# A fused two-block transformer on one core: stack DMAs by parts, banks of maxima and x moved, and the order of the front and of self attention

## The reference

```
# block 0: cross attention with adaptive norm
xq  = (1+scale_q(cond)) * norm(x)   + bias_q(cond)
xkv = (1+scale_k(cond)) * norm(ctx) + bias_k(cond)
x   = x + mha(xq@Wq+bq, xkv@Wk+bk, xkv@Wv+bv) @ Wp + bp
# block 1: self attention, cross attention, MLP
h = norm(x)*(1+scale_msa) + shift_msa
x = x + (mha(q, k, v of h@qkv_w + qkv_b) @ self_o_w + self_o_b) * gate_msa
h = norm(x)*g2 + b2
x = x + mha(h@q_w+q_b, ctx@k_w+k_b, ctx@v_w+v_b) @ cross_o_w + cross_o_b
h = norm(x)*(1+scale_mlp) + shift_mlp
x = x + (gelu(h@w1+b1) @ w2 + b2) * gate_mlp
```

## Time and profile before

| what | value |
|---|---|
| time, median of 3 runs | 539.46 us (538.98 to 542.21) |
| the profiled execution | 543.47 us, span 541.7 us |
| mean granted TensorE clock | 0.911 |
| busy share: PE, VectorE, ScalarE, GpSimd | 85%, 54%, 46%, 34% |
| first exp of attention 0 | about 57.7 us |
| first cross layer | 57.7 to 257.5 us |
| self layer | 257.5 to 340.9 us |
| second cross layer | 340.9 to 482.1 us |
| MLP | 482.1 us to the end |

### The profile page before, as it was taken

The page is one execution under the profiler, slowest core; times in us unless marked ns, Lnnn a source line. Parts: engine busy times, 40 slices in busy tenths (PEclk is TensorE's granted clock), DMA queues, the critical chain, the costliest instruction groups (busy, mean ns, idle before and its releaser), DMA issues.

```text
span 541.7 us, 11662 instructions
## 1 busy us (share of the span) xinstructions
PE 457.9 (85%) x4306; PEld 325.8 (60%) x4306; DVE 290.5 (54%) x784; ACT 250.3 (46%) x555; POOL 183.7 (34%) x245
## 2 busy tenths in 40 slices
PE   5765778989899879879797867898988987999996
PEld 5532454657575456556665644566656655678995
DVE  7717447471847544633766738745653543644321
ACT  1442455643555536555442323566665654572221
POOL 3233133463245425525141404244333413243200
PEclk9968698987999979999886868999999989999999
DMA  8667953472334275656817020746174032110000
GB/s 227 163 109 113 220 119 74 104 152 68 52 96 82 57 127 92 89 90 84 111 50 90 10 44 19 191 111 100 33 119 92 17 73 85 30 45 17 19 17 18
DMA packets 48927, 46.13 MB, mean 85 GB/s; under 512 B 12767, under 2 KB 47071, under 8 KB 48871
## 3 DMA queue, kind: packets, MB, share of 16 engines
q1 hardware_dynamic: 45951, 45.12, 42.8%
q10 hardware_dynamic: 2920, 0.27, 0.5%
HBM read 14.57 MB, written 0.93 MB: 29 GB/s over the span
## 4 chain that ended last, share of the span: by engine, by line
PE 60%; DVE 12%; issue 12%; ACT 6%; DMA 4%; POOL 3%; SPq 2%; ACTq 0%; POOLq 0%; DVEq 0%
PE bank L443 8%; PE bank L451 7%; DVE nmax L929 7%; PE bank L582 7%; PE bank L545 6%; PE bank L562 6%; PE bank L477 5%; PE bank L633 5%; PE bank L622 5%; PE bank L607 2%; PE bank L595 2%; ACT xt L683 2%; PE bank L500 2%; ACT prob L774 2%; DMA q_stack_all<-nm_t 2%
## 5 line engine op out<-in xcount | busy, mean ns | idle before, releaser
L929 DVE TENSOR_REDUCE nmax<-bank 112x1 f32<-112x375 f32 (+1 forms) x288 | 141.9, 549 | 101.8 <-PE bank L545 101.1
L774 ACT ACTIVATE prob<-bank 128x448 f32<-128x448 f32 (+2 forms) x224 | 116.4, 544 | 80.0 <-PE bank L562 75.5
L545 PE MATMUL bank<-k_stack,q_stack_all 96*128 96x375 bf16 x256 | 68.1, 350 | 24.0 <-issue 10.8
L1068 POOL TENSOR_TENSOR fill_space<-fill_space 128x375 f32<-128x375 f32 x32 | 29.9, 934 | 117.3 <-ACT fill_space L706 117.3
L562 PE MATMUL bank<-q_stack_all,k_stack 99*128 99x112 bf16 x768 | 55.7, 217 | 7.0 <-DMA q_stack_all<-nm_t 6.9
L451 PE MATMUL bank<-wkv,fill_space 128*128 128x256 f32 (+1 forms) x192 | 53.2, 418 | 9.5 <-ACT xt L683 7.1
L545 PEld LDWEIGHTS bank<-k_stack,q_stack_all 96*128 96x128 bf16 x256 | 24.6, 103 | 58.1 <-DVE nmax L929 21.8
L443 PE MATMUL bank<-fill_space,wkv 128*128 128x375 f32 x128 | 54.6, 555 | 3.1 <-ACT fill_space L706 2.3
L582 PE MATMUL bank<-prob,v_tokens 128*17 128x112 f32 (+1 forms) x1536 | 57.0, 266 | 0.1
L562 PEld LDWEIGHTS bank<-q_stack_all,k_stack 99*128 99x128 bf16 x768 | 41.7, 100 | 24.7 <-issue 13.4
L1082 POOL TENSOR_TENSOR v_tokens<-v_tokens,bias_rows_v 128x256 f32<-128x256 f32 (+1 forms) x48 | 33.5, 713 | 44.4 <-ACT v_tokens L718 44.4
(11 more groups left out here) (120 smaller groups left out, 687.9 us busy)
## 6 DMA issues: line engine op xcount, KB each, us to landing
k_stack<-fill_space SPq DMA_DIRECT2D x192, 93.8 KB, 3.5
q_stack_all<-q_part SPq DMA_DIRECT2D x72, 112.0 KB, 4.2
k_stack_all<-ctx_norm SPq DMA_DIRECT2D x24, 112.0 KB, 5.0
k_stack_all<-in_L_xcond_mlp_w_dram SPq DMA_DIRECT2D x2, 1024.0 KB, 7.8
...
```

Of the source, the lines that this page charges most:

```text
L545: last = pe.matmul(to[:, o:o + w], q_all[0:DEEP, q + h * N2:q + h * N2 + P], keys, start=True, stop=True)
L774: act.activation(prob[n % 4][0:rows, :], bank[SCORE_T[n % 2]][0:rows, 0:GH * T], ACT.Exp).then_inc(exp_done, 1)
L929: dve.tensor_reduce(nmax[:, g * hs:(g + 1) * hs], bank[SCORE[n % 3]][0:T, 0:hs * w].rearrange("t (h k) -> t h k", k=w), AX_X, ALU.max, neg ...
L1068: pool.tensor_tensor(kr[:, m, :], kf[:, m, :], kp[i % 2][:, 0, m, :], ALU.subtract).then_inc(krest_done, 1)
```

## The change

Five edits, none of which adds or drops arithmetic:

1. load_k and d wait part by part: the three DMAs of the high part go once the high part is there, then the two of the middle, then the low one.
2. In a cross attention the steps k stand at units 3 and 5 instead of 4 and 6, and D of half 0 at unit 6 instead of 7.
3. X of pairs 2 to 5 goes from bank CX to TB, at unit 7 instead of 6 (behind V in the list).
4. The maxima's transpose (all but those of attentions 10 to 15) goes into the score bank that is next in the ring; PE waits until that bank's group before has been read, and the next group in it waits for the maxima's copy.
5. The front is reordered and some of its T and K steps get banks 0, 1 and 3; loads 4 (contexts 4 to 7) comes before D(1). In the self layer X, Q, Kp, Vp, h, m, d of pair 7 come later, those of pair 8 earlier; B(9) one place earlier.

```diff
@@ -130,13 +130,13 @@
...
     for n, s in enumerate([
-            [("A", 0), ("cA", 0), ("order", -1), ("B", 0), ("cB", 0), ("mods", 0), ("mods", 1), ("X", 0), ("T", 0, 0), ("T", 0, 1),
-             ("order", 0), ("A", 1), ("cA", 1), ("B", 1), ("cB", 1)],
-            [("Q", 0), ("K", 0, 0), ("h", 0, "q"), ("K", 0, 1), ("m", 0, "q"), ("k", 0, 0), ("k", 0, 1), ("X", 1), ("T", 1, 0), ("T", 1, 1),
-             ("d", 0, "q"), ("D", 0, 0), ("D", 0, 1), ("cA", 2)],
+            [("A", 0), ("cA", 0), ("order", -1), ("B", 0), ("mods", 0), ("X", 0), ("cB", 0), ("mods", 1), ("Q", 0), ("T", 0, 0), ("T", 0, 1),
+             ("order", 0), ("h", 0, "q"), ("A", 1), ("cA", 1), ("m", 0, "q"), ("B", 1), ("cB", 1)],
+            [("K", 0, 0), ("K", 0, 1), ("k", 0, 0), ("k", 0, 1), ("X", 1), ("T", 1, 0), ("T", 1, 1),
+             ("d", 0, "q"), ("D", 0, 0), ("D", 0, 1), ("loads", 4), ("cA", 2)],
...
-             ("n", 0), ("d", 1, "q"), ("loads", 4)],
+             ("n", 0), ("d", 1, "q")],
             [("T", 2, 0), ("N", 0), ("L", 0), ("T", 2, 1), ("cA", 3)]]):
@@ -152,8 +152,8 @@
...
                     put(a, u, "K", i + 2, u // 2)
-                if u in (4, 6) and i + 2 < 2 * B:
-                    put(a, u, "k", i + 2, (u - 4) // 2)
+                if u in (3, 5) and i + 2 < 2 * B:
+                    put(a, u, "k", i + 2, (u - 3) // 2)
                 if u in (7, 9) and i + 1 < 2 * B:
@@ -171,7 +171,7 @@
...
                     put(a, u, "cB", i + 3)
-                if u in (7, 12) and i + 2 < 2 * B:
+                if u in (6, 12) and i + 2 < 2 * B:
                     put(a, u, "D", i + 2, u // 12)
@@ -186,25 +186,25 @@
...
-    (1, 2): [("A", 2)], (1, 4): [("B", 2)], (1, 6): [("X", 2)], (1, 9): [("Q", 2)], (1, 11): [("h", 2, "q")],
+    (1, 2): [("A", 2)], (1, 4): [("B", 2)], (1, 7): [("X", 2)], (1, 9): [("Q", 2)], (1, 11): [("h", 2, "q")],
     (2, 0): [("m", 2, "q")], (2, 3): [("d", 2, "q")],
-    (2, 2): [("A", 3)], (2, 4): [("B", 3), ("order", 1)], (2, 6): [("X", 3)], (2, 9): [("Q", 3)], (2, 11): [("h", 3, "q"), ("mods", 2)],
+    (2, 2): [("A", 3)], (2, 4): [("B", 3), ("order", 1)], (2, 7): [("X", 3)], (2, 9): [("Q", 3)], (2, 11): [("h", 3, "q"), ("mods", 2)],
     (3, 0): [("m", 3, "q")], (3, 3): [("d", 3, "q")],
-    (3, 2): [("A", 4)], (3, 4): [("B", 4)], (3, 6): [("X", 4)], (3, 9): [("Q", 4)], (3, 11): [("h", 4, "q")], (3, 12): [("Kp", 4)],
+    (3, 2): [("A", 4)], (3, 4): [("B", 4)], (3, 7): [("X", 4)], (3, 9): [("Q", 4)], (3, 11): [("h", 4, "q")], (3, 12): [("Kp", 4)],
...
     (5, 0): [("h", 4, "k")], (5, 2): [("m", 4, "k"), ("A", 5)], (5, 5): [("d", 4, "k")],
-    (5, 4): [("B", 5)], (5, 6): [("X", 5)], (5, 9): [("Q", 5)], (5, 11): [("h", 5, "q")], (5, 12): [("Kp", 5)],
+    (5, 4): [("B", 5)], (5, 7): [("X", 5)], (5, 9): [("Q", 5)], (5, 11): [("h", 5, "q")], (5, 12): [("Kp", 5)],
...
     (8, 4): [("A", 7)],
-    (9, 0): [("B", 7)], (9, 1): [("X", 7)], (9, 2): [("Q", 7)], (9, 4): [("Kp", 7), ("h", 7, "q")],
-    (10, 0): [("h", 7, "k")], (10, 1): [("Vp", 7), ("m", 7, "q"), ("d", 7, "q")], (10, 2): [("m", 7, "k"), ("d", 7, "k")],
-    (11, 0): [("A", 8)], (11, 2): [("B", 8)], (11, 4): [("X", 8)], (12, 2): [("Q", 8)], (12, 4): [("h", 8, "q")],
-    (13, 1): [("m", 8, "q"), ("d", 8, "q")],
-    (13, 0): [("A", 9)], (13, 2): [("B", 9)], (13, 4): [("X", 9)],
+    (9, 0): [("B", 7)], (9, 3): [("X", 7)], (10, 0): [("Q", 7)], (10, 2): [("Kp", 7), ("h", 7, "q")],
+    (10, 3): [("h", 7, "k")], (10, 4): [("Vp", 7), ("m", 7, "q"), ("d", 7, "q")], (11, 0): [("m", 7, "k"), ("d", 7, "k"), ("A", 8)],
+    (11, 1): [("B", 8)], (11, 3): [("X", 8)], (12, 0): [("Q", 8)], (12, 2): [("h", 8, "q")],
+    (12, 4): [("m", 8, "q"), ("d", 8, "q")],
+    (13, 0): [("A", 9)], (13, 1): [("B", 9)], (13, 4): [("X", 9)],
@@ -217,13 +217,15 @@
...
 BANK_OF = {("X", 0): 0, ("Q", 0): 1, ("X", 1): 2, ("Q", 1): 3, ("mods", 0): 7, ("mods", 1): TB,
-              ("Q", 2): TB, ("Q", 3): TB, ("Q", 4): TB, ("Kp", 4): TB, ("Q", 5): TB, ("Kp", 5): TB, ("Q", 10): TB, ("Q", 11): TB}
+              ("T", 0, 1): 3, ("K", 0, 1): 0, ("T", 1, 1): 3, ("K", 1, 1): 1,
+              ("X", 2): TB, ("Q", 2): TB, ("X", 3): TB, ("Q", 3): TB, ("X", 4): TB, ("Q", 4): TB, ("Kp", 4): TB,
+              ("X", 5): TB, ("Q", 5): TB, ("Kp", 5): TB, ("Q", 10): TB, ("Q", 11): TB}
...
-    uses, filled, read, maxima, tails = {}, {}, {}, {}, 0
+    uses, filled, read, maxima, tails, groups, ring = {}, {}, {}, {}, 0, 0, {}
@@ -236,20 +238,24 @@
...
-            elif step[0] == "N" and B + 2 <= step[1] <= 2 * B:
+            elif step[0] == "S":
+                groups += step[3] - step[2]
+            elif step[0] == "N" and B + 2 <= step[1] < 2 * B:
                 uses[step] = (CX, filled[CX], read[CX], 0, maxima.get(CX, 0), 0)
                 maxima[CX] = step[1] + 1
-            elif step[0] == "N" or step[0] == "tail" and step[2] == 0:
+            elif step[0] == "N":
+                uses[step] = (SCORE[groups % 3], 0, 0, 0, 0, 0)
+                ring[groups] = step[1] + 1
+            elif step[0] == "tail" and step[2] == 0:
                 uses[step] = (TB, filled.get(TB, 0), read.get(TB, 0), 0, maxima.get(TB, 0), tails)
-                maxima[TB] = step[1] + 1 if step[0] == "N" else maxima[TB]
             tails += step[0] == "tail" and step[2] == 2
-    uses["tail", NA - 1, 0] = (TB, filled[TB], read[TB], 0, maxima[TB], tails)
+    uses["tail", NA - 1, 0] = (TB, filled[TB], read[TB], 0, maxima.get(TB, 0), tails)
     for n in (13, 14, 15):
         use(("X", n), jobs_in(n))
-    return uses, filled, read
-USES, FILLED, READ = count_uses()
+    return uses, filled, read, ring
+USES, FILLED, READ, RING = count_uses()
@@ -439,6 +445,8 @@
...
                 pe.wait_ge(wkv_ordered, CH * (i // B + 1))
+                if USES["T", i, 1][0] != bk:
+                    read_by(pe, ("T", i, 1))
             for c in range(CH):
@@ -509,6 +517,8 @@
...
             a = step[1]
+            if bk in SCORE:
+                wait(pe, max_done, [g for g in RING if RING[g] >= a + 1][0] - 2)
             pe.wait_ge(nm_step, 4 * a + 4)
@@ -537,6 +547,7 @@
...
             wait(pe, max_done, n - 2)
+            wait(pe, nm_done, RING.get(n, 0))
             to = bank[SCORE[n % 3]]
@@ -943,7 +954,7 @@
...
             wait(dve, nm_in[a % 2], 16 * (a // 2))
-            src = cx[0:3 * H, CH * T:CH * T + T // 2].bitcast(BF16)
+            src = bank[USES[step][0]][0:3 * H, CH * T:CH * T + T // 2].bitcast(BF16)
             dve.tensor_copy(nm_t[a % 2][:, :], src).then_inc(nm_done, 1)
@@ -1061,7 +1072,7 @@
...
             _, i, m = step
-            pool.wait_ge(read[CX], USES[step][2] + 1)
+            read_by(pool, step)
             wait(pool, ksplit[m], 3 * i)
@@ -1151,13 +1162,20 @@
...
     def load_k(eng, i, half):
-        for m in range(CH):
-            eng.wait_ge(ksplit[m], 3 * (i + 1))
         lo, hi = half * P // HB, (half + 1) * P // HB
         at, to = half * H // HB * L, (half + 1) * H // HB * L
-        for s, w in enumerate(TERMS_K):
-            eng.dma_start(k_st[i % 2][s * D:(s + 1) * D, at:to].rearrange("d (h n) -> d h n", n=CH * L),
-                          kp[i % 2][lo:hi, w, :, :].rearrange("p c n -> p (c n)")).then_inc(kstacked[i % 2][half], 16)
+        for w in range(3):
+            if w == 0:
+                for m in range(CH):
+                    read_by(eng, ("K", i, m))
+            elif w == 1:
+                eng.wait_ge(kmid_done, CH * (i + 1))
+            else:
+                for m in range(CH):
+                    eng.wait_ge(ksplit[m], 3 * (i + 1))
+            for s in [s for s in range(NTERM) if TERMS_K[s] == w]:
+                eng.dma_start(k_st[i % 2][s * D:(s + 1) * D, at:to].rearrange("d (h n) -> d h n", n=CH * L),
+                              kp[i % 2][lo:hi, w, :, :].rearrange("p c n -> p (c n)")).then_inc(kstacked[i % 2][half], 16)
@@ -1174,12 +1192,12 @@
...
             to, terms = (q_all, TERMS_Q) if k == "q" else (k_all, TERMS_K)
-            sp.wait_ge(low_done[k], kinds_no(n, k) + 1)
             if k == "q" and l > 0:
...
                 sp.wait_ge(filled[CX], USES["gates", 0][1] + 1)
-            for t, w in enumerate(terms):
+            for w, t in [(w, t) for w in range(3) for t in range(NTERM) if terms[t] == w]:
+                sp.wait_ge((high_done, mid_done, low_done)[w][k], kinds_no(n, k) + 1)
```

## The result

The changed kernel takes 523.09 us (median of 4 runs, 520.37 to 526.35) against 539.22 us of the kernel before, a ratio of 0.969 (0.962 to 0.977). The forecast was 498 us, 487 to 517. The gain is 16 us, not 41. The profiled execution took 521.28 us, its span is 519.5 us. Medians are of all runs and ratios of those within 1.5% of the fastest; the profiled executions of experiments 3 and 12 were not among these, so their stage times lie high.

A forecast was written before the change was run, and what follows sets the result against it. TensorE was taken as nearly the bound, with time to win only from its idle gaps and its clock. Gains of 13.3 + 4.3 + 12.2 + 12.8 + 4.5 - 2.0 = 45.1 us off 543.5 gave 498 us, range 487 to 517.

The forecast's parts named there:

- Half 0's parts: Second cross layer: earlier stack DMAs end five score waits, 8.2 us, and give back 5.1 us of clock, 13.3 in all.
- k one place up: Conversions ahead of exp 4 and exp 6 delay them in each of 14 attentions: a cost of 2 us, bounds 0 and 7.
- The slower rival: ScalarE stalls on k at unit 5, waiting for a late GpSimd difference: time 552, chance 0.04.
- Attention 1's wait of 2.60 us: First cross layer, wait at 76.78: goes as the stack leaves earlier, 4.3 us with its clock.
- Half 1: K stack's second half lands at +4.5 us, its reader head 8 comes at +5.2 at the earliest: 0.7 us of room.
- I leave it so: Front: the maxima's DMA, 5.82 us from 51.28 with SyncE's queue full, was kept at that length.
- 4.5 us for the new order: Front: new step order and banks start stack DMAs about three us earlier; gain 4.5 us, bounds 2 and 7.
- The self layer: Pair 7's move gains 5.7 and loses 1.0 us, pair 8's gains 4.7 of wait and 3.4 of clock: 12.8.
- The terms for pair 7's move: Self layer: x's 2.33 us wait and 3.4 of clock go, 5.7 us; a later stack loses 1.0.
- The banks: x in the tail's bank ends four waits of V on xt, 7.1 us plus 5.1 of clock: 12.2; maxima's transpose at nothing.
- The second rival: Self-layer scores wait 4 us for pair 7's stack, clock falls, half 1's room is short: 9 us, time 507, chance 0.15.
- The first rival: Waits go but the clock does not come back, half clock falls elsewhere: 18.7 us lost, time 517, chance 0.16.

The follow-up runs named there:

- experiment 3: Kernel before plus only the stack DMAs waiting part by part, k at units 3 and 5, and D of half 0 at unit 6: 522.84 us, 0.970.
- experiment 12: The kernel of experiment 11 plus, in attention 22, head 8 of the next scores one unit later: 503.12 us, 0.934 of the kernel before.
- experiment 15: The kernel of experiment 12 with k back at units 4 and 6 and the first D at unit 7: 501.72 us, 0.934 of the kernel before.
- experiment 4: Kernel before plus only the stack DMAs waiting part by part, no step moved: 525.88 us, 0.974.
- experiment 5: Kernel before with only loads 4 moved in front of D(1): 543.5 us, 1.010.
- experiment 2: Changed kernel, loads 4 at its old place but waiting for attention 0's maxima to land, MLP weights for attention 16's: 519.37 us, 0.967 of the kernel before.
- experiment 11: Changed kernel, old self-layer order, only context 4 early, d(1) and contexts 5-7 behind attention 0's maxima, loads 1 and 2 later, MLP weights behind attention 16's: 505.42 us.
- experiment 10: Kernel before plus only the front's new order and its T and K banks, loads 4 at its old place: 537.78 us, 0.998.
- experiment 14: The kernel of experiment 12 with the front's order and its T and K banks as in the kernel before: 502.2 us, 0.934 of the kernel before.
- experiment 8: Changed kernel with the self-layer steps of pairs 7, 8 and 9 at their old places: 515.68 us, 0.959 of the kernel before.
- experiment 9: Changed kernel with pair 7's self-layer steps at their old places, pairs 8 and 9 at the new: 518.21 us, 0.965 of the kernel before.
- experiment 13: The kernel of experiment 12 with x of pairs 2 to 5 back at unit 6 in the bank shared with V: 510.73 us, 0.945 of the kernel before.

## Why the prediction was wrong, step by step

**Half 0's parts: right.** All five waits of 8.2 us are gone, DMAs leave as worked out (6.7 us from the attention's head, forecast 7.5), and the clock of the stretches behind them is back. The waits at the heads of attentions 17 to 22 are in no kernel that has the parts.

**k one place up: 2.0 forecast, not to be seen.** Experiment 15 against 12, and 3 against 4, lie within each other's intervals, which would hide a cost of this size. The slower rival, ScalarE stalled by GpSimd, did not come up.

**Attention 1's wait of 2.60 us: right.** By the parts alone the attention takes 4.4 us less (experiment 4), forecast 4.3; after, with the banks, it takes 21.0 us instead of 27.5. That the whole first cross layer comes within 0.9 us of its forecast is luck in part: PE's idle time fell by 6.3 us where 9.7 were forecast, and its busy time, by the clock, fell by 8.3 where 6.8 were.

**Half 1: the next wait in line, right in place, wrong in where it decides.** The text gave it 0.7 us of room and took it at no cost. In attentions 17 to 21 that holds. In 22, which has no K to make for a later context, the first units run faster: head 8's scores come at +3.8 us, the half lands at +5.1. The wait is 1.35 us, and 3.4 us of work is lost to half clock around it. Experiment 12 gives back 1.9 us of attention 22. This and the maxima of attention 16 are why the clock of the layer stays at 0.96, one of the prediction's signs of being wrong.

**The front: the step that failed most.** It is "I leave it so": the 5.82 us of the maxima's DMA was taken over as a constant, and it became 11.72. That number was read correctly as a wait behind SyncE's full queue; but the edits change just that queue. Loads 4 go early (experiment 5: 11.56 us, and 5.5 us slower by itself), and even without that the parts let SyncE run ahead, so that the contexts' loads get in front of the maxima (experiment 4: 9.14 us). This is 5.9 us at attention 0. The 7 us for the loads' transfer and the landing of D(1) by 53 were wrong with it: beside the stack DMAs the contexts' packets ran from 36.4 to 51.0, and the last packet of D(1) went at 58.2. No engine waited for that stack itself, but the maxima stood behind it. At attention 16 the same cause costs 3.0 us in attention 15 and 2.3 in 16 (34.0 to 28.7 in experiments 2 and 11). The other half of the step, 4.5 us for the new order, was 0.6 (experiments 10 and 14): the walk took away PE's wait for the bank and did not ask whether VectorE, behind it, had the time. It had work for 9.4 of the 10 us, and PE waited 4.4 us for it.

**The self layer: 12.8 forecast, 5.7 measured.** The terms for pair 8 are about right and come by the parts alone (experiment 4: attention 14 is 6.8 us shorter, forecast 8.1). The same parts took 3.7 us off attention 12, by an earlier stack of pair 7 in the old order, where the text kept a loss. The terms for pair 7's move have the wrong sign. The wait of 2.33 us for x went, yet the step did not name what queues behind B(7) on VectorE: B(7) kept its place ahead of N and the maxima, and with x later PE reaches the next scores first and waits 2.73 us for them. Q(7) and Q(8) stand ahead of N in the shared bank, which costs 0.88 us twice, behind ScalarE's q_full. All the moves together cost 4.4 us of the stage, 7 of the median (experiment 8); how they share it is open (experiment 9). The 1.0 us for a late stack of pair 7 didn't come.

**The banks: 12.2 forecast, 7.6 to 9 by the medians.** In the four attentions it is 8.1 to 10.8 us (experiment 13 against 11, 12, 14 and 15). The waits for xt are nearly as large as stated (7.1 us before, 6.2 in experiment 13), and the 5.1 us of clock lie within what the profiles show (3.1 to 6.6 in these attentions). What was put at nothing is the maxima's transpose: without the wait for xt PE comes to it sooner, VectorE's last split of the maxima doesn't, and PE waits 0.71, 0.52 and 0.52 us for it in attentions 1, 2 and 3, none of which is there before or in experiment 13. The term was also read from a profile with more half clock than the median run: alone on the kernel before, the edit gave 5.7 us (2.6 to 8.8).

**The sum.** Maxima's DMAs 5.9 + 3.0 + 2.3 = 11.2, the front's order 3.9, the self layer's order 4.4, half 1 about 2: 21.5 of the 22.9 us between the span forecast (496.6) and the span of after (519.5). The front's order is a gain that never was; the other three have repairs. With all three (experiment 15) the span is 501.8 us, without that for half 1 (experiment 11) 502.3, 5 to 6 us from the forecast. That these kernels come so near is luck in part: their maxima's DMA takes 2.4 us, where the forecast kept 5.8, and their self layer of 70.9 to 73.9 us has the old order, where the forecast's 70.6 was for the new.

**The rivals.** The second rival (a new wait in the self layer and at half 1, 9 us) is near in size, 4.4 + 2, but the cause that it names in the self layer is a late stack, and the runs show late maxima: near by luck. None of them had the maxima's DMA, though its row stood in the prediction, costed as a constant. The first rival, whose 517 us is the nearest of all to the result, is not what happened: where the waits went, the clock came back (0.96 from 0.92 in the first cross layer after the change, 0.99 in the second of experiment 11).

By the Trainium skill (DMA: Bandwidth & Descriptors, Queues, rings and completion order) each DMA engine changes between the queues it has work for, a packet at a time, so the backlog of SyncE's queue would not hold up ScalarE's. The runs disagree: the first packet of attention 0's maxima came 1.5 us after its issue with the queue empty, 3.4 with stack DMAs in it, 4.1 with the contexts' loads 0.8 us behind as well (experiment 10), and 6.7 to 8.1 with these loads issued 0.4 to 17 us ahead. Small DMAs do not always do it: before, two of q's stack DMAs went out in the 1.0 us ahead of attention 16's maxima, whose first packet came after 1.5 us. Whether this is the packets themselves, their descriptors, or something ahead of the DMA engines, no run here shows.
